# A vision block with attention and routed FFN on one core: joint rotation of two tiles, FFN groups of three chunks, three dispatch scatters in flight, nine serial search rounds

## The chip, the cores and the metric

The kernel runs on one core of one Trainium2 chip. The metric is the device time of one execution in microseconds (us), the median of several runs. Engines are named TensorE (PE; PEld is its weight load), VectorE (DVE), ScalarE (ACT), GpSimd (POOL) and SyncE (SP).

## The reference

64 images of 224 x 224 x 3 become 196 patches each, 12544 tokens of width D = 192. The block embeds the patches, adds attention, and adds an FFN with one shared expert and eight routed ones:

```python
h = patches(x) @ W + b                          # 768 -> 192
n = layernorm(h); q, k = rope(n @ Wq.T), rope(n @ Wk.T); v = n @ Wv.T    # 12 heads of 16
w = where(tril, erf(q @ k.T / 4) + 1, 0)        # per image, 196 x 196
h = h + (w @ v / max(w.sum(-1), 1e-6)) @ Wproj.T
f = layernorm(h); probs = softmax(f @ Wr); top 2 of 8, their weights normalized
capacity = ceil(12544 * 2 / 8 * 1.25)           # the best `capacity` tokens of each expert
routed  = scatter_add(order, (silu(f[order] @ w1) * (f[order] @ w3)) @ w2 * weight)
shared  = (silu(f @ s1) * (f @ s3)) @ s2        # inner width 768
return h + routed + shared
```

`rope` turns neighbouring pairs of a head's 16 channels by an angle that depends on the position.

## The kernel before

The program has three parts in a row, each with its own stream of instructions per engine, written by hand, with semaphores between them; no scheduler moves anything.

**attention()** goes over 32 units of two images (392 tokens, four tiles of 98 rows). Within a unit `turn()` goes over steps n = 0 to 11, one per pair of heads: TensorE makes the scores, ScalarE copies them (L420) and applies gelu (L435), VectorE forms the weights (L549, L556, L608, L564), GpSimd multiplies (L690), TensorE sums over v. Between these steps the next unit is prepared: ScalarE copies the transposed, normalized tokens `normed_t` at n = 3 (L411, behind the gelu of that step), TensorE multiplies tokens of the unit after it (L748) and then q and k of the next (L741), ScalarE copies these to `qk_raw` (L411), and VectorE rotates two of the four tiles at n = 3 and two at n = 4 (L617 to L636). The sum with the projection is at L653, and the bias of the tokens is added once per unit at L663. `by_cos` and `by_sin` hold the products of one tile; two of each take turns. VectorE instructions that read what VectorE wrote just before are set apart by `settle()`, a wait on its own semaphore.

**choices()** does the routing: the top two, and for each expert a search for the threshold at its capacity, in ROUNDS = 15 rounds of three trials. A round is three counts on VectorE (L1069), their sum over the chunks on TensorE (L1052), and the comparison (L926, L1094). SERIAL of the rounds run alone, ahead of the FFN; the rest, a count, and the placing of the tokens (from step PLACING = 18 to step 23) run as steps s of `search_and_place` on VectorE, one behind each pair of inner chunks of the first ROUTING = 5 shared units, beside `add_counts` on TensorE. `R.total` and `R.offset` are its PSUM banks. The last two steps add to `R.placed`.

**ffn()** goes over 25 shared units g of 512 tokens (the last, SHORT, 256) and then 64 routed units of 490 tokens, eight per expert. The inner width 768 is MI = 6 chunks m of 128. `tensor_pair` makes gate and up of two chunks: eight ordinary passes per chunk (L1245 to L1248, float16 in high and low parts), and then the passes of half the rows for both chunks (L1251 and L1253, which run side by side). `tensor_out`, a third of the down projection of the unit before (L1274 to L1276), follows each pair. ScalarE does silu and the high part of hidden (`scalar_unit`, L1290, L1284), VectorE the product and the low part (`vector_unit`, L1309, L1302). `split` prepares tokens of a later unit at chunk `split_at`: for shared units 3, for SHORT and the routed ones 1. Gate and up have two PSUM banks each, so pair p + 1 needs the banks that pair p's chunks leave:

```python
for m in (2 * pair, 2 * pair + 1):
    pe.wait_ge(T.multiplied, MI * g + m + 1)
```

GpSimd writes each token's place into a table by 196 indirect DMAs (L1464), as soon as `R.placed` is 2, with at most two in flight; SyncE loads `ids` from that table after all of them, and GpSimd gathers the rows of the routed units by `ids` (L1476), which `split` (ScalarE L1576, VectorE L1661) turns into high and low parts that a DMA transposes.

## Time and profile before

| | before |
|---|---|
| runs, us | 3378.82, 3384.44, 3385.17 (median 3384.44) |
| profiled execution, us | 3376.83 |
| its span, us | 3374.7 |
| mean granted TensorE clock | 0.945 |
| TensorE busy | 3091.8 us (92%), 25828 instructions |
| VectorE busy | 2446.8 us (73%), 4893 instructions |
| ScalarE busy | 1526.7 us (45%) |
| GpSimd busy | 1377.0 us (41%) |
| chain that ended last | TensorE 44%, VectorE 2%, ScalarE 1%, issue 2% |

Attention takes the span's first 1600 us or so, the serial part of the routing the next hundred, the shared units reach to about 2200 and the routed ones to the end. The busy shares are means over these stages. A row of a timeline gives the start, the duration, the engine, the line, the operation, what is written and read, its form, and in brackets how long the engine was idle before it and what ended that. A row of the waits gives who waited for whom, for how long in total, how often, and the longest. A row of the windows gives the window and its length, then the busy time and the instructions of PE, PEld, DVE, ACT and POOL, then the granted clock, the busy share of the DMA engines and GB/s. The granted clock is given as a share of full speed.

### The profile page before, as it was taken

Reading aid. Unit: us, or ns where it says so; the run is one execution under the profiler, and the core shown is the slowest. Engines: PE = TensorE matmul, PEld = TensorE weight load, DVE = VectorE, ACT = ScalarE, POOL = GpSimd, SP = SyncE. Lnnn points to the kernel's source line nnn. Section 1 sums busy time; section 2 is a strip of 40 time slices with the busy share of each in tenths; the row PEclk is TensorE's granted clock in tenths of the full one; section 3 lists DMA queues with packets and bytes.
Section 4 is the critical chain, followed back from the end, with each engine's and each line's share of the span. In section 5 each row is a group of like instructions: output and inputs, shape, how many; then the busy total and the mean of one; then the engine's idle time right before and its main releaser. Section 6 shows DMA issues by size and latency. Waiting matters only on the chain. (4 is left out here: it accounts for less than half of the span.)

```text
span 3374.7 us, 70939 instructions
## 1 busy us (share of the span) xinstructions
PE 3091.8 (92%) x25828; PEld 2110.6 (63%) x25828; DVE 2446.8 (73%) x4893; ACT 1526.7 (45%) x3223; POOL 1377.0 (41%) x1172
## 2 busy tenths in 40 slices
PE   6999999999999999998059999899999999999997
PEld 5777777777777777766025555556666556566664
DVE  6999999999999999997766555554555455455543
ACT  2444444444444444443024444444555455455443
POOL 1332233223332332322202555536666555655664
PEclk9899999999999999986579999999999999999999
DMA  3333333323332333322122222245554555545442
GB/s 104 77 75 78 73 87 80 81 66 87 89 76 68 81 89 75 75 46 54 45 67 67 74 67 78 59 95 101 77 96 71 98 71 97 101 69 97 77 75 42
DMA packets 460505, 260.36 MB, mean 77 GB/s; under 512 B 337967, under 2 KB 441759, under 8 KB 456063
## 3 DMA queue, kind: packets, MB, share of 16 engines
q1 hardware_dynamic: 392448, 196.41, 24.3%
q0 software_dynamic: 54464, 49.01, 10.3%
q10 hardware_dynamic: 13262, 10.66, 0.9%
q8 instruction: 192, 3.15, 0.4%
q14 instruction: 139, 1.14, 0.1%
HBM read 107.98 MB, written 68.15 MB: 52 GB/s over the span
## 5 line engine op out<-in xcount | busy, mean ns | idle before, releaser
L1309 DVE SCALAR_TENSOR_TENSOR ffn_hidden<-ffn_up,ffn_silu 128x490 f32<-128x490 f32 (+2 forms) x534 | 350.6, 670 | 676.2 <-ACT ffn_silu L1290 510.9
L690 POOL TENSOR_TENSOR weights<-weights,x_pair 128x400 f32<-128x400 f32 x384 | 396.3, 1032 | 828.7 <-DVE weights L556 810.1
L1290 ACT ACTIVATE ffn_silu<-ffn_gate 128x490 f32<-128x490 f32 (+2 forms) x534 | 301.9, 582 | 735.6 <-PE ffn_up L1253 541.6
L1487 POOL DMA_INDIRECT out_rows<-done,ids x256 | 407.4, 1591 | 407.6 <-ACT done L1593 346.4
L608 DVE RECIPROCAL recip<-x_product 128x200 f32<-128x200 f32 x384 | 534.2, 1391 | 0.0
L1274 PE MATMUL ffn_out<-ffn_w_hi,ffn_hidden_hi 128*128 128x192 f16 (+1 forms) x2124 | 525.6, 247 | 3.9 <-DVE ffn_hidden_lo L1302 2.0
L1275 PE MATMUL ffn_out<-ffn_w_lo,ffn_hidden_hi 128*128 128x192 f16 (+1 forms) x2124 | 522.8, 246 | 0.0
L1276 PE MATMUL ffn_out<-ffn_w_hi,ffn_hidden_lo 128*128 128x192 f16 (+1 forms) x2124 | 522.7, 246 | 0.0
L748 PE MATMUL bank<-w_tok,patches 128*128 128x192 f32 x1536 | 327.2, 370 | 56.8 <-ACT normed_t L411 32.7
L1302 DVE TENSOR_TENSOR ffn_hidden_lo<-ffn_hidden,ffn_hidden_hi 128x490 f16<-128x490 f32 (+2 forms) x534 | 356.3, 667 | 15.9
L1284 ACT CAST ffn_hidden_hi<-ffn_hidden 128x490 f16<-128x490 f32 (+2 forms) x534 | 320.7, 601 | 91.9 <-DVE ffn_hidden L1309 90.7
L748 PEld LDWEIGHTS bank<-w_tok,patches 128*128 128x128 f32 x1536 | 290.4, 217 | 72.8 <-ACT normed_t L411 39.2
L1476 POOL DMA_INDIRECT tokens<-dram_x,ids x256 | 279.1, 1090 | 91.1 <-issue 76.2
L420 ACT ACTIVATE x_pair<-score 128x400 f32<-128x400 f32 x384 | 192.5, 502 | 269.2 <-DVE weights L556 180.4
L857 PE MATMUL y_sum<-v_held,weights 128*64 128x68 f32 (+1 forms) x1536 | 262.4, 253 | 31.5 <-DVE weights L564 31.5
L1274 PEld LDWEIGHTS ffn_out<-ffn_w_hi,ffn_hidden_hi 128*128 128x128 f16 (+1 forms) x2124 | 219.2, 103 | 110.3 <-issue 98.5
L1464 POOL DMA_INDIRECT dram_table<-entry,slot_of x196 | 202.9, 1035 | 207.4 <-issue 131.8
L435 ACT ACTIVATE weights<-x_pair 128x400 f32<-128x400 f32 x384 | 205.0, 534 | 182.0 <-PE y_sum L863 177.5
L741 PE MATMUL bank<-w_qkv,normed_t 96*128 96x192 f32 (+1 forms) x1024 | 275.5, 418 | 0.7 <-ACT normed_t L411 0.7
L859 PE MATMUL y_sum<-v,weights 128*64 128x51 f32 (+2 forms) x1536 | 248.3, 244 | 0.0
L1245 PE MATMUL ffn_gate<-ffn_tokens,ffn_w_hi 128*128 128x490 f16 (+2 forms) x534 | 199.8, 374 | 36.3 <-DVE ffn_tokens L1230 12.4
L741 PEld LDWEIGHTS bank<-w_qkv,normed_t 96*128 96x128 f32 x1024 | 180.3, 192 | 68.9 <-issue 4.4
(176 smaller groups left out, 6862.2 us busy)
## 6 DMA issues: line engine op xcount, KB each, us to landing
patches<-in_patches SPq DMA_DIRECT2D x32, 1176.0 KB, 5.2
ffn_raw<-in_w SPq DMA_DIRECT2D x18, 768.0 KB
dram_x_t<-x_t SPq DMA_DIRECT2D x32, 392.0 KB, 3.7
x_t<-dram_x_t SPq DMA_DIRECT2D x24, 512.0 KB
base<-dram_h SPq DMA_DIRECT2D x24, 384.0 KB, 4.2
out_rows<-sums ACTq DMA_DIRECT2D x24, 384.0 KB, 4.6
v_held<-v SPq DMA_DIRECT2D x64, 102.0 KB, 2.3
dram_h<-h SPq DMA_DIRECT2D x32, 192.0 KB
```

What stands on the lines that cost most here:

```text
L608: nc.vector.reciprocal(recip[:, n % 2], x_product[:, n % 2]).then_inc(inverted, 1)
L690: nc.gpsimd.tensor_tensor(weights[:, n % 4], weights[:, n % 4], x_pair[:, n % 4, ::-1], ALU.mult)\
L741: last = nc.tensor.matmul(out, wide(lhs, k, t), rhs[:, k, 0:width], start=(k == 0), stop=(k == 1))
L748: last = nc.tensor.matmul(out, wide(patches[slot], i, n), tok_w[:, i, :], start=(i == 0), stop=(i == KP - 1))
L1274: nc.tensor.matmul(out, hi, w_hi[:, m, :], start=(m == 0), stop=False)
L1275: nc.tensor.matmul(out, hi, w_lo[:, m, :], start=False, stop=False)
L1276: last = nc.tensor.matmul(out, lo, w_hi[:, m, :], start=False, stop=(m == MI - 1))
L1284: nc.scalar.copy(T.hidden_hi[slot][:, m, 0:n], T.hidden[:, m % 2, 0:n]).then_inc(T.hi_ready, 1)
L1290: nc.scalar.activation(T.silu[:, m % 2, 0:n], T.gate[m % 2][:, 0:n], ACT.Silu, scale=1.0 / (TOKEN_SCALE * WEIGHT_SCALE)).then_inc(T.silued, 1)
L1302: nc.vector.tensor_tensor(T.hidden_lo[slot][:, m, 0:n], T.hidden[:, m % 2, 0:n], T.hidden_hi[slot][:, m, 0:n], ALU.subtract).then_inc(T.lo ...
L1309: nc.vector.scalar_tensor_tensor(T.hidden[:, m % 2, 0:n], T.up[m % 2][:, 0:n], HIDDEN_SCALE / (TOKEN_SCALE * WEIGHT_SCALE), T.silu[:, m % ...
L1487: nc.gpsimd.indirect_dma_start(out=dram["out"][:, :], out_offset=bass.IndirectOffsetOnAxis(ap=ids[i][0:height, t, 0:1], axis=0), in_=done[ ...
```

## The change

Six edits:

- **Rotation.** `by_cos` and `by_sin` hold both tiles of a step. Both copies of `qk_raw` are waited for, then one product by cosine and one by sine cover both tiles, then one difference and one sum.
- **Copies ahead of gelu.** At n = 3 ScalarE copies `normed_t` before the gelu of the step.
- **SERIAL** is 9 instead of 11, so that steps 9 to 23 lie behind the 15 pairs of units 0 to 4.
- **Groups.** `tensor_group` and `units_group` take three chunks where no routing step stands (from unit 5 on); gate and up have a third bank each, `R.total` and `R.offset`. Unit 5 waits for `R.placed` first. The down projection comes in halves there, the last one of all in one part. Seven shared units are written out instead of five.
- **Split.** In units with groups of three it stands at chunk 2 (shared), at chunk 5 (SHORT), and ahead of chunk 0 (routed).
- **Dispatch.** FLYING = 3 scatters may be in flight.

```diff
-        by_cos = [sb(f"by_cos{s}", [128, 2 * NH, 2, HD // 2]) for s in range(2)]
-        by_sin = [sb(f"by_sin{s}", [128, 2 * NH, 2, HD // 2]) for s in range(2)]
+        by_cos = sb("by_cos", [128, 2, 2 * NH, 2, HD // 2])
+        by_sin = sb("by_sin", [128, 2, 2 * NH, 2, HD // 2])
...
+                    if n == 3 and has_next:
+                        for k, pos in enumerate(LN1T):
+                            copy_out(pos, normed_t[:, k * UT:(k + 1) * UT], KD)
                     if pairs:
...
                         nc.scalar.activation(weights[:, n % 4], x_pair[:, n % 4], ACT.Gelu, scale=SCORE_SCALE)\
                           .then_inc(gelued, 1)
-                    if n == 3 and has_next:
-                        for k, pos in enumerate(LN1T):
-                            copy_out(pos, normed_t[:, k * UT:(k + 1) * UT], KD)
...
-                        shape = [128, 2 * NH, 2, HD // 2]
+                        t = 2 * (n - 3)
                         for i in range(2):
-                            t = 2 * (n - 3) + i
-                            dve.wait_ge(free[QK[t] % NB], fills(kind, u, QK[t]))
-                            src = qk_raw[:, t, :].rearrange("p (h c f) -> p h c f", h=2 * NH, c=2)
-                            if i == 0:
-                                settle()
-                            step(nc.vector.tensor_tensor(by_cos[i][:], src, over(tables[:, i, 0, :], shape), ALU.mult))
-                            step(nc.vector.tensor_tensor(by_sin[i][:], src, over(tables[:, i, 1, :], shape), ALU.mult))
+                            dve.wait_ge(free[QK[t + i] % NB], fills(kind, u, QK[t + i]))
                         settle()
-                        for i in range(2):
-                            t = 2 * (n - 3) + i
-                            step(nc.vector.tensor_tensor(rotated[:, t, :, 0:HD // 2], by_cos[i][:, :, 0, :],
-                                                         by_sin[i][:, :, 1, :], ALU.subtract))
-                            step(nc.vector.tensor_tensor(rotated[:, t, :, HD // 2:HD], by_cos[i][:, :, 1, :],
-                                                         by_sin[i][:, :, 0, :], ALU.add))
+                        src = qk_raw[:, t:t + 2, :].rearrange("p i (g f) -> p i g f", f=HD // 2)
+                        for c, out in enumerate((by_cos, by_sin)):
+                            table = tables[:, :, c, :].unsqueeze(2).to_broadcast([128, 2, 4 * NH, HD // 2])
+                            step(nc.vector.tensor_tensor(out[:].rearrange("p i h c f -> p i (h c) f"), src, table, ALU.mult))
+                        settle()
+                        step(nc.vector.tensor_tensor(rotated[:, t:t + 2, :, 0:HD // 2], by_cos[:, :, :, 0, :],
+                                                     by_sin[:, :, :, 1, :], ALU.subtract))
+                        step(nc.vector.tensor_tensor(rotated[:, t:t + 2, :, HD // 2:HD], by_cos[:, :, :, 1, :],
+                                                     by_sin[:, :, :, 0, :], ALU.add))
...
-SERIAL = 11
+SERIAL = 9
...
+FLYING = 3
...
+    T.gate.append(R.total)
+    T.up.append(R.offset)
...
+def units_group(g):
+    return 2 if isinstance(g, int) and g < ROUTING else 3
...
+def tensor_group(nc, pe, T, g, slot, ws, n, part, group):
+    chunks = range(group * part, group * part + group)
+    after_pairs = group == 3 and isinstance(g, int) and g == ROUTING
...
-        pe.wait_ge(T.multiplied, MI * g + m + 1)
+        pe.wait_ge(T.multiplied, MI * g + m + 3 - (2 if after_pairs and m < 2 else group))
...
-    share = len(tiles) * MI // 3
-    for k in range(third * share, (third + 1) * share):
+    share = len(tiles) * MI // parts
+    for k in range(part * share, (part + 1) * share):
...
+    if split_at is None:
+        split()
...
-                if n >= 2:
-                    pool.wait_ge(dispatched[n % 2], 16 * (n // 2))
+                if n >= FLYING:
+                    pool.wait_ge(dispatched[n % FLYING], 16 * (n // FLYING))
...
+                if isinstance(g, int) and g == ROUTING:
+                    pe.wait_ge(R.placed, 2)
+                group = units_group(g)
...
-            for part in range(3):
-                tensor_out(nc, pe, T, SHARED + XUNITS - 1, 0, 0, ROUTED, part)
+            tensor_out(nc, pe, T, SHARED + XUNITS - 1, 0, 0, ROUTED, 0, 1)
```

Where the change moves instructions, the order on the engine is shown before and after. On VectorE, one of the two rotation places of a unit, before:

```order
L626 TENSOR_TENSOR by_cos<-qk_raw,rope 128x384
L627 TENSOR_TENSOR by_sin<-qk_raw,rope 128x384
L626 TENSOR_TENSOR by_cos<-qk_raw,rope 128x384
L627 TENSOR_TENSOR by_sin<-qk_raw,rope 128x384
L631 TENSOR_TENSOR rotated<-by_cos,by_sin 128x24x8
L633 TENSOR_TENSOR rotated<-by_cos,by_sin 128x24x8
L631 TENSOR_TENSOR rotated<-by_cos,by_sin 128x24x8
L633 TENSOR_TENSOR rotated<-by_cos,by_sin 128x24x8
L549 SCALAR_TENSOR_TENSOR x_product<-x_pair 128x200
```

The same place after:

```order
L627 TENSOR_TENSOR by_cos<-qk_raw,rope 128x768
L627 TENSOR_TENSOR by_sin<-qk_raw,rope 128x768
L629 TENSOR_TENSOR rotated<-by_cos,by_sin 128x48x8
L631 TENSOR_TENSOR rotated<-by_cos,by_sin 128x48x8
L549 SCALAR_TENSOR_TENSOR x_product<-x_pair 128x200
```

Four instructions stand where eight stood, and the elements they cover are the same. On ScalarE, step n = 3 of a unit (`h_new` are the raw tokens, `x_pair` the scores), before:

```order
L420 ACTIVATE x_pair<-score 128x400
L435 ACTIVATE weights<-x_pair 128x400
L411 COPY normed_t<-bank 96x392 x2
L411 COPY h_new<-bank 128x192
L411 COPY qk_raw<-bank 128x384 x2
```

And after (L438 is the gelu now):

```order
L420 ACTIVATE x_pair<-score 128x400
L411 COPY normed_t<-bank 96x392 x2
L438 ACTIVATE weights<-x_pair 128x400
L411 COPY h_new<-bank 128x192
L411 COPY qk_raw<-bank 128x384 x2
```

The two copies passed the gelu. On TensorE, the end of a pair in a routed unit, before:

```order
L1248 MATMUL ffn_up<-ffn_tokens,ffn_w_hi 128x490
L1251 MATMUL ffn_gate<-ffn_tokens,ffn_w_lo 128x490
L1253 MATMUL ffn_up<-ffn_tokens,ffn_w_lo 128x490
L1251 MATMUL ffn_gate<-ffn_tokens,ffn_w_lo 128x490
L1253 MATMUL ffn_up<-ffn_tokens,ffn_w_lo 128x490
L1274 MATMUL ffn_out<-ffn_w_hi,ffn_hidden_hi 128x192
```

The end of a group after (`total` and `offset` are the third banks of gate and up):

```order
L1261 MATMUL offset<-ffn_tokens,ffn_w_hi 128x490
L1264 MATMUL ffn_gate<-ffn_tokens,ffn_w_lo 128x490
L1266 MATMUL ffn_up<-ffn_tokens,ffn_w_lo 128x490
L1264 MATMUL ffn_gate<-ffn_tokens,ffn_w_lo 128x490
L1266 MATMUL ffn_up<-ffn_tokens,ffn_w_lo 128x490
L1264 MATMUL total<-ffn_tokens,ffn_w_lo 128x490
L1266 MATMUL offset<-ffn_tokens,ffn_w_lo 128x490
L1287 MATMUL ffn_out<-ffn_w_hi,ffn_hidden_hi 128x192
```

Three chunks' half-row passes stand together; there are two such ends per unit instead of three.

## Rows read from the trace of the kernel before

**Rows 1.** Windows: busy time of each engine in two stages.

```profile
200.00:1500.00 1300.00, 1230.93 (x11933) 953.23 (x11931) 1253.14 (x2807) 616.34 (x1410) 393.32 (x381) 0.96 0.33 78
...
2200.00:3300.00 1100.00, 1091.86 (x8070) 657.04 (x8071) 564.92 (x903) 555.82 (x1123) 642.45 (x480) 1.00 0.49 86
```

**Rows 2.** Timeline of VectorE, the rotation of a unit.

```profile
836.06 0.55 DVE L626 TENSOR_TENSOR by_cos<-qk_raw,rope 128x384 f32<-128x384 f32 x1
836.52 0.55 DVE L627 TENSOR_TENSOR by_sin<-qk_raw,rope 128x384 f32<-128x384 f32 x1
...
838.04 0.36 DVE L631 TENSOR_TENSOR rotated<-by_cos,by_sin 128x192 f32<-128x192 f32 x1
838.32 0.35 DVE L633 TENSOR_TENSOR rotated<-by_cos,by_sin 128x192 f32<-128x192 f32 x1
```

**Rows 3.** Timeline of VectorE, one instruction per unit of attention, 128x768.

```profile
821.59 0.95 DVE L663 TENSOR_TENSOR h_new<-h_new,bias 128x768 f32<-128x768 f32 x1
...
868.71 0.94 DVE L663 TENSOR_TENSOR h_new<-h_new,bias 128x768 f32<-128x768 f32 x1
...
917.16 0.95 DVE L663 TENSOR_TENSOR h_new<-h_new,bias 128x768 f32<-128x768 f32 x1
```

**Rows 4.** Timeline of ScalarE, in two units of attention.

```profile
835.09 0.48 ACT L411 COPY qk_raw<-bank 128x384 f32<-128x384 f32 x1 [0.81 <-PE bank L741]
...
876.41 0.53 ACT L435 ACTIVATE weights<-x_pair 128x400 f32<-128x400 f32 x1
...
883.62 0.48 ACT L411 COPY qk_raw<-bank 128x384 f32<-128x384 f32 x1 [0.81 <-PE bank L741]
```

**Rows 5.** Timeline of VectorE, the rotation one unit later.

```profile
883.16 0.55 DVE L626 TENSOR_TENSOR by_cos<-qk_raw,rope 128x384 f32<-128x384 f32 x1
```

**Rows 6.** Waits in attention, 300 to 1400 us (23 units): total, times, longest.

```profile
PE bank L748 <- ACT normed_t L411: 27.6, 23, 1.3
...
DVE h L653 <- PE bank L741: 11.1, 20, 0.6
```

**Rows 7.** Windows at the token products of two units; PEclk is the granted clock.

```profile
829.00:834.00 5.00, 3.83 (x20) 3.08 (x19) 4.93 (x11) 2.10 (x6) 1.95 (x2) 1.00 0.66 241
876.80:880.40 3.60, 3.04 (x10) 3.05 (x11) 3.53 (x8) 0.89 (x3) 1.25 (x2) 0.53 0.69 290
```

**Rows 8.** Timeline of TensorE, two serial search rounds.

```profile
1657.41 0.56 PE L1052 MATMUL total<-count,same 128*128 128x3 f32 x2 [54.33 <-DVE reached L1069]
1662.53 0.59 PE L1052 MATMUL total<-count,same 128*128 128x3 f32 x2 [4.56 <-DVE reached L1069]
```

**Rows 9.** Timeline of VectorE, a search round behind a pair, and what follows.

```profile
1726.11 0.15 DVE L926 TENSOR_SCALAR enough<-total 128x3 int32<-128x3 f32 x1
...
1730.47 0.69 DVE L1309 SCALAR_TENSOR_TENSOR ffn_hidden<-ffn_up,ffn_silu 128x512 f32<-128x512 f32 x1
```

**Rows 10.** Timeline of TensorE, shared unit 2, behind its third pair.

```profile
1782.60 0.39 PE L1057 MATMUL offset<-running,before 128*128 128x8 f32 x2 [3.05 <-DVE running L1076]
```

**Rows 11.** Timeline of TensorE, end of a pair in a routed unit.

```profile
2604.05 0.37 PE L1247 MATMUL ffn_up<-ffn_tokens,ffn_w_lo 128*128 128x490 f16 x1
2604.26 0.37 PE L1248 MATMUL ffn_up<-ffn_tokens,ffn_w_hi 128*128 128x490 f16 x1
2604.56 0.38 PE L1251 MATMUL ffn_gate<-ffn_tokens,ffn_w_lo 64*128 64x490 f16 x1
...
2605.08 0.26 PE L1274 MATMUL ffn_out<-ffn_w_hi,ffn_hidden_hi 128*128 128x192 f16 x1
```

**Rows 12.** The dispatch scatters on GpSimd: ns, first and last start.

```profile
L1464 POOL DMA_INDIRECT dram_table<-entry,slot_of x196: 969/972/1760, 1816.0 to 2178.6; - x196
```

**Rows 13.** Timeline of ScalarE, the last shared unit (SHORT).

```profile
2191.15 0.63 ACT L1576 ACTIVATE split_rows<-tokens 128x512 f16<-128x512 f32 x1 [7.90 <-DMA tokens<-dram_x,ids]
```

**Rows 14.** Timeline of TensorE, the SHORT unit, and the last unit of all.

```profile
2193.75 0.28 PE L1245 MATMUL ffn_gate<-ffn_tokens,ffn_w_hi 128*128 128x256 f16 x1 [4.36 <-issue]
...
3347.31 0.24 PE L1274 MATMUL ffn_out<-ffn_w_hi,ffn_hidden_hi 128*128 128x192 f16 x1 [1.82 <-DVE ffn_hidden_lo L1302]
```

More of the change, by code:

```diff
@@ L1164, in ffn_weights, with ffn_units @@
     return T
[L1167 removed]
+def ffn_units(ctx, nc, T, R):
     def sb(name, shape, dt=F32):
@@ L1248, in tensor_pair, with tensor_out @@
             nc.tensor.matmul(out, hi[:, beyond], far, start=False, stop=False)
-    for m in (2 * pair, 2 * pair + 1):
+    for m in chunks:
         beyond = slice(INNER + m * 128, INNER + (m + 1) * 128)
-        nc.tensor.matmul(T.gate[m % 2][:, 0:n], T.w_lo[ws][0][top, beyond], far[top], start=False, stop=True)\
+        nc.tensor.matmul(T.gate[m % group][:, 0:n], T.w_lo[ws][0][top, beyond], far[top], start=False, stop=True)\
           .then_inc(T.gated, 1)
-        nc.tensor.matmul(T.up[m % 2][:, 0:n], T.w_lo[ws][1][low, beyond], far_again[low], start=False, stop=True)\
+        nc.tensor.matmul(T.up[m % group][:, 0:n], T.w_lo[ws][1][low, beyond], far_again[low], start=False, stop=True)\
           .then_inc(T.gated, 1)
-def tensor_out(nc, pe, T, g, slot, ws, tiles, third):
-    if third == 0:
+def tensor_out(nc, pe, T, g, slot, ws, tiles, part, parts):
+    if part == 0:
         pe.wait_ge(T.lo_ready, MI * g + MI + 2)
@@ L1299, in vector_unit @@
 def vector_unit(nc, dve, T, g, slot, n, split, split_at, behind_pair=None):
+    group = units_group(g)
     def lo(m):
@@ L1303, in lo @@
                                 ALU.subtract).then_inc(T.lo_ready, 1)
+    if split_at is None:
+        split()
     for m in range(MI):
@@ L1321, in shared_units @@
 def shared_units(eng, unit):
-    for g in range(ROUTING):
+    ahead = ROUTING + 2
+    for g in range(ahead):
         unit(g, g // 2, g % 2, WHOLE)
-    with eng.Fori(0, (SHARED - 2 - ROUTING) // 2) as j:
-        unit(2 * j + ROUTING, j + ROUTING // 2, 1, WHOLE)
-        unit(2 * j + ROUTING + 1, j + ROUTING // 2 + 1, 0, WHOLE)
+    with eng.Fori(0, (SHARED - 2 - ahead) // 2) as j:
+        unit(2 * j + ahead, j + ahead // 2, 1, WHOLE)
+        unit(2 * j + ahead + 1, j + ahead // 2 + 1, 0, WHOLE)
     unit(SHARED - 2, (SHARED - 3) // 2, 1, WHOLE)
@@ L1378, in ffn @@
                 "xt_in", "base_in", "sums_out", "rows_in", "scattered", "routed_in"))
-        dispatched = [sem(f"dispatched{k}") for k in range(2)]
+        dispatched = [sem(f"dispatched{k}") for k in range(FLYING)]
         ids_in = [sem(f"ids_in{i}") for i in range(8)]
@@ L1414, in _ @@
                 sp.dma_start(ids[i][XR:XR16, 3, :], dram["pads"]).then_inc(pads_in, 16)
-            for k in range(2):
-                sp.wait_ge(dispatched[k], 16 * PER)
+            for k in range(FLYING):
+                sp.wait_ge(dispatched[k], 16 * len(range(k, 2 * PER, FLYING)))
             for i in range(4):
@@ L1529, in unit @@
                 pe.wait_ge(T.tokens_lo, 2 * g + 6)
-                for part in range(3):
-                    tensor_pair(nc, pe, T, g, slot, 0, columns_of(tiles), part)
+                if isinstance(g, int) and g == ROUTING:
+                    pe.wait_ge(R.placed, 2)
+                group = units_group(g)
+                for part in range(MI // group):
+                    tensor_group(nc, pe, T, g, slot, 0, columns_of(tiles), part, group)
                     if isinstance(g, int) and g < ROUTING:
@@ L1534, in unit @@
                     if not (isinstance(g, int) and g == 0):
-                        tensor_out(nc, pe, T, g - 1, 1 - slot, 0, WHOLE, part)
+                        tensor_out(nc, pe, T, g - 1, 1 - slot, 0, WHOLE, part, MI // group)
             shared_units(pe, unit)
```

33 lines of the change are left out of this document (16 added, 17 removed).

## The prediction

> **What bounds the kernel now.** I read the busy shares of the engines by stage first, then each stage's longest engine in the timeline, then who waits for whom. The kernel has three stages with different limits [rows 1]. In attention (200 to 1500 us) VectorE is busy 1253 of 1300 us and TensorE 1231: VectorE leads, TensorE is close behind. In the routed units (2200 to 3300) TensorE is busy 1092 of 1100, and VectorE has half its time free. Between the two lie the routing and the first shared units, where TensorE stands and VectorE's search sets the pace [rows 8 to 10]. So the parts of the change pay by different rules: an instruction saved on VectorE counts in attention, a pass saved on TensorE counts in the FFN, a serial round counts whole.
>
> The profiled execution took 3376.83 us; the median of the three runs, 3384.44, lies 7.6 above it. The sum is made in differences, which I put on the median. Two measurements of this kernel cannot tell less than about 0.2% (6.8 us) from no change.
>
> **Rotation on VectorE.** Before, one of the two rotation places of a unit is four products of 384 elements and four sums of 192. Products start 0.46 apart though each is 0.55 long, so the next starts before the last is done; sums start 0.28 apart [rows 2]. Afterwards there are two products of 768 and two sums of 384. The trace has an instruction of 768 elements, 0.945 long [rows 3]; less the same overlap it takes about 0.86. So two products turn from 0.93 into 0.86 and two sums from 0.55 into 0.47: 0.15 per pair of instructions merged, and with two such merges (cosine and sine; difference and sum) 0.30 per place, 0.60 per unit. That is the gain where VectorE never waits.
>
> It does wait in every other unit. Units alternate: 821.59 to 868.71 is 47.1, 868.71 to 917.16 is 48.5 [rows 3]. In the long kind TensorE's granted clock is 0.53 around the token products, against 1.00 at the same place of the short kind [rows 7], and VectorE then waits for the projection; over 23 units these waits are 11.1 us in 20 pieces [rows 6]. In a long unit what VectorE saves becomes more of that wait. What shortens it is the other edit in attention: ScalarE copies the normalized tokens ahead of the gelu instead of behind it. TensorE waits for those copies once per unit, 27.6 us over 23 units, 1.2 each [rows 6]; the gelu in front takes 0.53, less the tenth by which ScalarE's instructions overlap [rows 4]. So the long unit gains about 0.4. The gelu comes later by two copies; GpSimd, its user, then waits for VectorE's weights anyway, so I cost that at nothing.
>
> The merged product needs both copies of qk_raw at its start, where before the first was enough. In the short kind the second copy ends at 835.57 and VectorE comes at 836.06 [rows 2, 4]: no wait. In the long kind it ends at 884.10 and VectorE came at 883.16 [rows 4, 5]: a new wait of 0.94, less the 0.4 by which the copies come earlier, 0.5. What is queued behind it on VectorE is the rest of the unit, up to the projection's sum, where 0.5 is what it has waited anyway. So I take it as absorbed.
>
> Mean gain (0.6 + 0.4)/2 = 0.5 for each of 31 units that prepare a next one: **-16**. Bounds: -40 where both kinds gain fully, +7 where all units become the long kind less 0.4 (48.05 against a mean of 47.8).
>
> The VectorE rows weigh against a rule. The Trainium skill, page "VectorE: DVE Perf Modes", section "The DRAIN you can't avoid", says that the next instruction does not start until the pipe has emptied; its section on the TRN2 errata gives (N+151)/0.96 ns for a float32 tensor_tensor, so that each instruction removed would be worth 0.157 us, 0.63 per place and 1.26 per unit. The lengths in the trace agree with that formula, the starts do not agree with the first sentence.
>
> **Nine serial rounds instead of eleven.** A serial round is 5.12 us, with TensorE idle for 4.56 of it [rows 8]: 2 x 5.12 = 10.2 gone. The two rounds go behind pairs of a shared unit, where one costs VectorE 4.36 us [rows 9], between its own FFN work. Everything behind them slips by two pairs: placing starts in unit 3 instead of unit 2, and its last step lies behind unit 4's last pair. The stall for placing, 3.05 us [rows 10], should mostly go, since the placing then starts behind a unit's first pair, with no split of tokens ahead of it. Two new stalls come: about 3 us for the two extra full rounds, and a wait ahead of unit 5, because groups of three need the PSUM banks of the routing. VectorE's last placing step stands in front of that wait; behind the wait TensorE holds unit 5's first group, and ScalarE and VectorE wait for that. I take 4. Net given back 3.7, so **-6.5**; bounds -10 (all hidden) and -1.5 (both rounds fall fully on TensorE: 8.7).
>
> **Groups of three.** Ordinary passes start 0.21 apart. From the last of them to the first down product it is 0.82, with one ordinary and two half-row passes in it, 3 x 0.21 = 0.62: changing to half rows and back costs 0.20 per group [rows 11]. Groups: 5 x 3 for the units with routing and 84 x 2 for the others (20 shared, 64 routed), instead of 89 x 3. 84 fewer x 0.20 = **-16.8**. The down products and other passes stay in number. The cover of the rest: three chunks are 24 ordinary passes, 5 us of TensorE, and ScalarE (556 of 1100 us) and VectorE (565) are half free there [rows 1], so hidden should be ready in time; if it is not, each late chunk shows as a TensorE wait for ffn_hidden. Bounds: -20 to -8 (if half of it comes back as waits at group ends). The split of the next routed tokens moves to the head of the unit; it waits for gathered rows that today land before it is due, and TensorE has one whole group to work on meanwhile.
>
> **Three scatters in flight, and the way into the routed units.** The 196 scatters run from 1816 to 2178.6, 1.85 apart, of which the instruction itself takes 0.97 [rows 12]; GpSimd waits for landings the rest, and they end after the shared units. With three in flight the gap should fall to some 1.3 to 1.55, and they end 60 to 100 us earlier (196 times 0.3 to 0.5). What follows is short: ScalarE stands 7.90 for gathered rows [rows 13] and TensorE 4.36 in the SHORT unit [rows 14]. Those go. But the split now comes at that unit's last chunk, and the transposes behind it, covered today by what is left of SHORT, lie open. I take **-2** (-8 to +3). The last unit's down projection in one part lets TensorE run up to the last chunk; of its wait of 1.82 [rows 14] I take **-1**.
>
> Sum: -16 - 6.5 - 16.8 - 2 - 1 = -42.3. The profile should take about 3334, and the median 3384.4 - 42.3 = **3342**.
>
> **Rivals.**
> 1. *The clock fall of the long units disappears.* TensorE idles 0.4 less before the token products, and stays at 1.00 there. Then all units are of the short kind: 47.1 - 0.6 = 46.5 instead of 47.8, -40 over 31 units, 24 below my term: 3318. For it: only one kind shows the fall. Against: TensorE waits as long in both kinds, so that wait alone does not explain the fall. 0.20.
> 2. *VectorE's pipe empties between instructions*, so that a merge is worth 0.157 instead of 0.07: 1.26 x 31 = -39, also about 3319. The starts of rows 2 speak against it. 0.05. (By the rule named above.)
> 3. *Attention gives nothing.* TensorE is busy 95% there; if its chain bounds both kinds, or 0.5 of new wait eats the gain, only the FFN terms stay: -26, 3358. For it: TensorE's share. Against: in the short kind VectorE does not wait. 0.18.
> 4. *The merged rotation waits for the second copy in every unit* and the wait is not absorbed. Place: VectorE at the rotation; price 0.94 on a long unit: 48.45 - 0.4 + 0.94 = 49.0 in both kinds, +1.2 x 31 = +37, 53 above my term: 3395, slower. It decides once VectorE arrives more than 0.5 earlier than today in the short kind, which is that kind's slack [rows 2, 4]. 0.05.
> 5. *Dispatch was hidden anyway, and the boundary gets worse* (open transposes, split stuck at the head of units): +3 instead of -2, and the groups give 8 instead of 17: 3356. 0.07.
>
> **How the numbers follow.** My forecast has 0.45. The range goes from 3313 (rival 1 with the better end of the boundary) to 3366 (attention at its upper bound of +7 with the other terms as taken lies at 3365); only rival 4 and the joint ends of several terms lie outside. Faster by over 0.2%: 0.92, within 0.03, slower 0.05.
>
> **What would show it.** Rotation: eight instructions of rows 2 become four, at 0.86 and 0.47 start to start; the alternation 46.5 and 48.0; a wait before the long unit's products of about 0.5. Routing: nine serial rounds of 5.12; a TensorE wait of 3 to 5 us ahead of unit 5; no stall of 3 us in unit 2. Groups: six passes of half rows in a row, routed units 0.2 shorter (two groups in place of three). Dispatch: last scatter before 2120. Boundary: no ScalarE wait of 7.9 for rows, a TensorE wait for transposed tokens instead. I am wrong if a unit of attention takes over 47.8 in the mean, or if routed units show waits for ffn_hidden.

## The result, and the profile after

The changed kernel takes 3571.34 us (3559.75 to 3588.90 in four runs) against 3381.63 before: 1.0567 times as long, 95% interval 1.0517 to 1.0617. It is slower by 190, where 42 less was forecast.

| | before | after |
|---|---|---|
| profiled execution, us | 3376.83 | 3588.90 |
| its span, us | 3374.7 | 3587.1 |
| mean granted TensorE clock | 0.945 | 0.913 |
| TensorE busy | 3091.8 (92%) | 3134.0 (87%) |
| VectorE busy, instructions | 2446.8, 4893 | 2430.2, 4637 |
| end of attention (last sum over v) | 1583.3 | 1582.8 |
| start of shared unit 0 | 1716.4 | 1705.5 |
| start of shared unit 5 | 1823.4 | 1818.9 |
| start of shared unit 8 | 1878.1 | 2108.8 |
| start of the last shared unit, SHORT | 2170.2 | 2397.1 |
| start of the first routed unit | 2200.2 | 2427.6 |
| start of the last routed unit | 3327.6 | 3539.8 |

The starts are those of each unit's first gate matmul. From one row to the next the difference between the kernels is -0.5, -10.4, +6.4, +235.2, -3.8, +0.5 and -15.2: all of the loss lies in shared units 5, 6 and 7, which took 30.8, 167.2 and 91.9 us instead of 18.2. The windows of the changed kernel show that stretch as the third row (columns as in [rows 1]):

```profile
200.00:1500.00 1300.00, 1239.27 (x11968) 958.71 (x11967) 1243.36 (x2597) 617.61 (x1413) 393.86 (x382) 0.96 0.34 78
1800.00:1840.00 40.00, 33.21 (x233) 19.25 (x231) 23.16 (x39) 15.04 (x27) 13.94 (x14) 0.96 0.21 67
1840.00:2098.00 258.00, 75.07 (x205) 20.41 (x205) 18.84 (x30) 14.72 (x26) 179.69 (x182) 0.54 0.05 11
2098.00:2400.00 302.00, 302.00 (x2206) 182.59 (x2206) 166.93 (x265) 137.99 (x247) 0.97 (x1) 0.99 0.21 69
2500.00:3300.00 800.00, 793.74 (x5958) 492.00 (x5956) 413.61 (x658) 409.86 (x832) 472.57 (x362) 1.00 0.51 89
```

Around it TensorE is as busy as it was [rows 1]; in it, it is busy for 75 of 258 us at half clock, VectorE for 19, the DMA engines for 5%. GpSimd alone works on: it issues the dispatch scatters. Three of its rows, from the timeline:

```profile
1901.39 0.97 POOL L1488 DMA_INDIRECT dram_table<-entry,slot_of  x1 [0.30 <-issue]
1902.67 0.97 POOL L1488 DMA_INDIRECT dram_table<-entry,slot_of  x1 [0.30 <-issue]
1903.94 0.97 POOL L1488 DMA_INDIRECT dram_table<-entry,slot_of  x1 [0.30 <-issue]
```

They follow each other every 1.28 us for up to 24 in a row, where two in flight had a mean of 1.86 [rows 12] and came at most two in a row. With the pauses that GpSimd makes between these rows, its own semaphore and register instructions among them (60 of 366 beside the slow units take over 0.5 us, most of them 0.70 to 0.73, where they take 0.02 or 0.03 in e1_two below), the mean is 1.43. TensorE's timeline nearby:

```profile
1863.07 0.59 PE L1258 MATMUL ffn_gate<-ffn_tokens,ffn_w_hi 128*128 128x512 f16 x1 [2.21 <-issue]
1865.87 0.59 PE L1259 MATMUL ffn_gate<-ffn_tokens,ffn_w_hi 128*128 128x512 f16 x1 [2.21 <-issue]
1868.67 0.59 PE L1260 MATMUL ffn_gate<-ffn_tokens,ffn_w_lo 128*128 128x512 f16 x1 [2.21 <-issue]
1871.47 0.59 PE L1261 MATMUL ffn_gate<-ffn_tokens,ffn_w_hi 128*128 128x512 f16 x1 [2.21 <-issue]
```

These are ordinary passes of one chunk, 0.21 apart in [rows 11], here 2.80 apart, with no wait for data: "issue" alone. Of the 145 starts beside the scatters that come over 0.65 us after the one before, 127 lie close to 0.7, 1.4, 2.1 or 2.8. SyncE, which only issues DMAs, has one issue of 1.40 us that takes 0.37 after the last scatter (2098):

```profile
2047.30 1.40 SPq L1421 DMA_DIRECT2D base<-dram_h  x1
...
2112.17 0.37 SPq L1421 DMA_DIRECT2D base<-dram_h  x1
```

It has only four issues in the stretch, and the other three took 0.69, 0.37 and 0.01, so SyncE alone would show little.

TensorE's first such gap comes at 1837.7, 18 us after the first scatter (1819.8), beside the ninth of an unbroken row that began at 1827.3. The granted clock is still 1.00 then; it falls at 1842.4, behind the first three late starts.

The other parts, by their lines. The rotation, in a unit where VectorE waits (first two rows) and in one where it does not:

```profile
694.29 0.37 DVE L564 SCALAR_TENSOR_TENSOR weights<-weights,causal 128x264 f32<-128x264 f32 x1
695.43 0.96 DVE L627 TENSOR_TENSOR by_cos<-qk_raw,rope 128x768 f32<-128x768 f32 x1 [0.78 <-issue]
...
742.87 0.94 DVE L627 TENSOR_TENSOR by_cos<-qk_raw,rope 128x768 f32<-128x768 f32 x1
743.73 0.95 DVE L627 TENSOR_TENSOR by_sin<-qk_raw,rope 128x768 f32<-128x768 f32 x1
744.72 0.56 DVE L629 TENSOR_TENSOR rotated<-by_cos,by_sin 128x384 f32<-128x384 f32 x1
745.20 0.55 DVE L631 TENSOR_TENSOR rotated<-by_cos,by_sin 128x384 f32<-128x384 f32 x1
```

The merged products start 0.86 apart and the sums 0.48, as taken. The wait of 0.78 is for the second copy, which ScalarE ends at 695.35:

```profile
694.87 0.48 ACT L411 COPY qk_raw<-bank 128x384 f32<-128x384 f32 x1 [0.81 <-PE bank L739]
```

The waits in attention, 300 to 1400 us (total, times, longest), against [rows 6]:

```profile
PE bank L746 <- ACT normed_t L411: 13.8, 22, 0.8
...
DVE by_cos L627 <- issue: 10.8, 10, 1.7
...
DVE h L651 <- PE bank L739: 8.3, 13, 0.6
```

TensorE's wait for the normalized tokens is halved; a wait of VectorE at the rotation is new, 10.8 us in 10 units; the wait at the projection fell from 11.1 only to 8.3.

The first unit of the FFN and unit 5, where TensorE now waits 4.85 for the placing:

```profile
1705.46 0.59 PE L1258 MATMUL ffn_gate<-ffn_tokens,ffn_w_hi 128*128 128x512 f16 x1 [12.46 <-DVE ffn_tokens L1233]
...
1818.86 0.58 PE L1258 MATMUL ffn_gate<-ffn_tokens,ffn_w_hi 128*128 128x512 f16 x1 [4.85 <-DVE slot_of L1083]
```

The end of a group in a routed unit:

```profile
2800.00 0.37 PE L1261 MATMUL offset<-ffn_tokens,ffn_w_hi 128*128 128x490 f16 x1
2800.30 0.38 PE L1264 MATMUL ffn_gate<-ffn_tokens,ffn_w_lo 64*128 64x490 f16 x1
...
2800.72 0.37 PE L1264 MATMUL total<-ffn_tokens,ffn_w_lo 64*128 64x490 f16 x1
...
2801.03 0.26 PE L1287 MATMUL ffn_out<-ffn_w_hi,ffn_hidden_hi 128*128 128x192 f16 x1
```

The turn to half rows and back stays at 0.3 on each side, as in [rows 11], once per three chunks: routed units take 17.53 instead of 17.74, shared ones 18.02 instead of 18.23.

### The profile page after: what moved, and what is told of

Same layout as the page of the kernel before. It is cut to its first block, busy times and chain, and to the rows that moved or that the text cites. A ratio compares the mean times of both kernels' runs of the same rounds, so it can differ in the third digit from the quotient of the medians.

```text
span 3587.1 us, 70594 instructions
## 1 busy us (share of the span) xinstructions
PE 3134.0 (87%) x25828; PEld 2135.0 (60%) x25828; DVE 2430.2 (68%) x4637; ACT 1528.3 (43%) x3223; POOL 1351.9 (38%) x1172
## 4 chain that ended last, share of the span: by engine, by line
PE 43%; issue 6%; DVE 2%; ACT 1%; POOL 0%; DMA 0%; ACTq 0%; DVEq 0%; POOLq 0%
PE ffn_out L1287 5%; PE ffn_out L1288 5%; PE ffn_out L1289 5%; PE ffn_gate L1264 2%; PE ffn_gate L1258 2%; PE ffn_gate L1259 2%; PE ffn_up L1258 2%; PE ffn_gate L1261 2%; PE ffn_gate L1260 2%; PE ffn_up L1259 2%; PE ffn_up L1260 2%; PE ffn_up L1261 2%; PE offset L1261 1%; PE offset L1259 1%; PE total L1258 1%
## 5 line engine op out<-in xcount | busy, mean ns | idle before, releaser
L1332 DVE SCALAR_TENSOR_TENSOR ffn_hidden<-ffn_up,ffn_silu 128x490 f32<-128x490 f32 (+2 forms) x366 | 237.9, 670 | 721.0 <-ACT ffn_silu L1308 469.7
L1308 ACT ACTIVATE ffn_silu<-ffn_gate 128x490 f32<-128x490 f32 (+2 forms) x366 | 204.0, 582 | 913.9 <-PE ffn_up L1266 526.0
L1288 PE MATMUL ffn_out<-ffn_w_lo,ffn_hidden_hi 128*128 128x192 f16 (+1 forms) x2124 | 525.7, 247 | 46.6 <-issue 46.6
L1511 POOL DMA_INDIRECT out_rows<-done,ids x256 | 405.3, 1583 | 419.8 <-ACT done L1620 358.5
L1500 POOL DMA_INDIRECT tokens<-dram_x,ids x256 | 265.7, 1038 | 387.6 <-DMA ids<-dram_table 307.5
L438 ACT ACTIVATE weights<-x_pair 128x400 f32<-128x400 f32 x384 | 205.6, 536 | 182.0 <-PE y_sum L861 177.4
L1288 PEld LDWEIGHTS ffn_out<-ffn_w_lo,ffn_hidden_hi 128*128 128x128 f16 (+1 forms) x2124 | 219.9, 104 | 56.6 <-issue 56.5
L1289 PEld LDWEIGHTS ffn_out<-ffn_w_hi,ffn_hidden_lo 128*128 128x128 f16 (+1 forms) x2124 | 219.7, 103 | 56.9 <-issue 56.8
L1488 POOL DMA_INDIRECT dram_table<-entry,slot_of x196 | 194.6, 993 | 127.3 <-issue 122.2
```

The source lines that it names most:

```text
L1288: nc.tensor.matmul(out, hi, w_lo[:, m, :], start=False, stop=False)
L1289: last = nc.tensor.matmul(out, lo, w_hi[:, m, :], start=False, stop=(m == MI - 1))
L1500: nc.gpsimd.indirect_dma_start(out=rows[slot][0:height, t, :], out_offset=None, in_=dram["x2"][:, :], in_offset=bass.IndirectOffsetOnAxis( ...
L1511: nc.gpsimd.indirect_dma_start(out=dram["out"][:, :], out_offset=bass.IndirectOffsetOnAxis(ap=ids[i][0:height, t, 0:1], axis=0), in_=done[ ...
```

## The experiments

Theory R says that scatters which follow each other without a break slow the issue of the other engines. The rivals blame code that runs for the first time, the third PSUM bank, three in flight as such, or what the scatters write. In the table, "excess" is the time from the start of shared unit 5 to that of SHORT above 19 steady units (18.02 each, 18.23 where pairs stand); "step" is from the start of SHORT to the first routed unit. Starts of the scatters are from the timelines. "One" marks a version that ran once; scatters, excess and step are from one profile each. With nine serial rounds unit 5 takes 1.4 to 2.9 us more than a steady unit even where TensorE never falls behind, so an excess of that size does not show a loss by the scatters.

| run | scatters: first to last, mean distance | excess | step | time, us |
|---|---|---|---|---|
| before | 1816 to 2179, 1.86 | 0.4 | 30.0 | 3381.6 |
| changed | 1820 to 2098, 1.43 | 236 | 30.5 | 3571.3 |
| e1_two | 1805 to 2163, 1.84 | 3.0 | 35.6 | 3350.4 |
| e2_before_three | 1816 to 2090, 1.40 | 242 | 27.8 | 3615.7 (one) |
| e3_paced | 1808 to 2264, 2.34 | 2.9 | 134 | 3446.5 (one) |
| e4_late | 1894 to 2173, 1.43 | 238 | 29.6 | 3587.3 (one) |
| e5_spaced2 | 1805 to 2091, 1.46 | 183 | 29.8 | 3520.6 (one) |
| e6_spaced4 | 1809 to 2111, 1.55 | 143 | 29.7 | 3479.7 |
| e10_threes | 1809 to 2202, 2.02 | 1.6 | 72.3 | 3384.2 (one) |
| e12_nines | 1803 to 2131, 1.68 | 48 | 29.4 | 3376.8 |
| e13_sixes | 1814 to 2166, 1.80 | 4.5 | 29.6 | 3350.5 |
| e15_fives11 | 1803 to 2174, 1.90 | 0.0 | 43.4 | 3358.5 |
| e9_serial11 | 1801 to 2165, 1.87 | 0.7 | 35.3 | 3347.6 |
| e14_quarter | 1806 to 2080, 1.41 | 236 | 30.5 | 3573.3 (one) |
| e11_gather | 1807 to 2084, 1.42 | 237 | 30.0 | 3576.3 (one) |

**Two in flight.**

```diff
-FLYING = 3
+FLYING = 2
```

> The changed kernel with two scatters in flight, all else as changed. Theory R (scatters that follow each other every 1.28 us slow the other engines' issue; units 5 to 7 took 30.8, 167 and 92 us instead of 18): units 5 to 7 take 18 to 20 us each, the 236 us of excess go, and the time falls to about 3571 - 236 = 3335 to 3355, some 25 to 45 below before. Theory U (the cause is the code written out for units 5 and 6 or the third PSUM bank, and the scatters are bystanders): units 5 to 7 stay at 30 to 170 us and the time above 3520.

Measured 3350.35, ratio 0.9907 (0.9878 to 0.9937); units 5 to 7 took 19.6, 18.0 and 18.0. With the one number turned back the other five edits gain 32 us. The scatters' row (ns; first and last start):

```profile
L1488 POOL DMA_INDIRECT dram_table<-entry,slot_of x196: 964/971/1832, 1805.3 to 2163.4; - x196
```

**The kernel before with three in flight**, the same lines of GpSimd and SyncE as in the change, nothing else.

> The kernel before with three scatters in flight, nothing else. Theory R: scatters every 1.28 us from 1816 on, over within 280 us, and the shared units meanwhile take 30 to 170 us instead of 18.2; time 3550 to 3620. Theory U: shared units stay at 18.2, the scatters end near 2080, time within 10 us of before.

Measured 3615.7, units 5 and 6 at 147 and 132 us:

```profile
L1466 POOL DMA_INDIRECT dram_table<-entry,slot_of x196: 966/971/1225, 1815.9 to 2089.5; - x196
```

The scatters alone make the loss; it needs neither the written-out units nor the third bank nor the groups.

**A pause behind each scatter.**

```diff
...
+                nc.gpsimd.memset(pace[:], 0.0).then_inc(paced, 1)
+                pool.wait_ge(paced, n + 1)
+                pool.sem_inc(spacer, 1)
```

> The changed kernel, three scatters in flight, but a memset of 128x256 and a wait for it behind each scatter, so that they start some 1.7 us apart. If the rate of the scatters is what hurts: units 5 to 7 near 18 us, time 3335 to 3360. If the number allowed in flight hurts whatever the rate: units 5 to 8 take 30 to 170 us again, time above 3500.

The distance came out at 2.3, not 1.7, since the wait for the memset costs 0.97. No unit is slow. The scatters end 112 us after SHORT has begun, and the step of 134 us is TensorE waiting for them; so 3446 lies in neither range, though the units are as the rate has them.

**A later start.**

```diff
+            pool.wait_ge(T.lo_ready, MI * 9 + 2)
+            pool.sem_inc(spacer, 1)
```

> The changed kernel, three scatters in flight back to back, but the first one waits until shared unit 9 is done, when the loop over the shared units has been through its body once on every engine. Theory R: the units that lie beside the scatters are slow whatever code they run: three or four units of 30 to 170 us, total excess near 236 us, time 3550 to 3600. Theory F (only code that has to be fetched for the first time is slowed): the units stay at 18 us, the scatters end by about 2180, time 3340 to 3360.

The same excess, now in units 10 and 11 (168 and 104 us), in code that every engine had run before. The Trainium skill, page "Runtime: NRT & Kernel Launch", section "Instruction fetch mechanics", has each engine load its instructions in blocks by its own DMA queue, mostly hidden. Code loaded for the first time was therefore a suspect; this run clears it.

**Other instructions between the scatters.**

```diff
...
+                for _ in range(2):
+                    pool.sem_inc(paced, 1)
```

(e6_spaced4: `range(4)`.)

> The changed kernel, three scatters in flight, two register-like instructions of 0.08 us behind each scatter, so that they follow at 1.44 us instead of 1.28. Theory T (the other engines fall behind only where scatters come faster than something drains them, and the limit of two was the brake: its mean was 1.85): between 1.28 and 1.85 there is a threshold; if it lies above 1.44, units 5 to 7 take 30 to 170 us again and the time is above 3480; if below, they take 18 and the time is 3335 to 3355. Theory C (three allowed in flight hurts by itself): slow in either case.

> As the run before, with four such instructions, 1.6 us from scatter to scatter. Theory T: no slow unit (18.0 from unit 6 on), last scatter near 2120 instead of 2163, the step from shared to routed units 30 instead of 35.6, time 3340 to 3350, at or up to 6 below the version with two in flight (3350). Theory C: slow units, above 3480.

Both missed what they were made for. The median distance stayed at 1.28; the small instructions run ahead while GpSimd works on a scatter. The means of 1.46 and 1.55 come from pauses in between. The loss falls with the mean (183, 143), which suits both theories.

**Rows of three, nine, six and five.** GpSimd waits until all scatters before have landed, ahead of every third:

```diff
-                if n >= FLYING:
-                    pool.wait_ge(dispatched[n % FLYING], 16 * (n // FLYING))
-                    pool.sem_inc(spacer, 1)
+                if n >= FLYING and n % FLYING == 0:
+                    for k in range(FLYING):
+                        pool.wait_ge(dispatched[k], 16 * (n // FLYING))
+                        pool.sem_inc(spacer, 1)
```

The others wait like this ahead of every ninth, sixth or fifth, and keep the limit of three between these pauses.

> The changed kernel, three scatters back to back, then a wait until all three have landed, and so on: three in flight at their peak, but a mean distance near that of two in flight (1.8 to 2.0 us). Theory T (the mean rate decides; 1.55 us still cost 143 us, two in flight at 1.85 cost nothing): units 5 to 15 at 18 to 20 us, time 3345 to 3365. Theory C (a third scatter in flight is what hurts): units of 25 us and more wherever scatters run, time above 3450.

```profile
L1488 POOL DMA_INDIRECT dram_table<-entry,slot_of x196: 964/972/1831, 1809.3 to 2202.3; - x196
```

```profile
1850.00:2050.00 200.00, 200.00 (x1464) 120.48 (x1463) 111.69 (x176) 92.80 (x165) 97.99 (x97) 1.00 0.24 74
```

TensorE is busy for all of 1850 to 2050. Three in flight do no harm when a pause follows; theory C falls. The pauses are too many, so the scatters end at 2202, the routed units wait, and 3384 misses theory T's range.

> The changed kernel, three scatters in flight, but ahead of every ninth scatter a wait until all before it have landed (about 3 us). Theory B (the other engines fall behind only after an unbroken row of scatters: TensorE's first gaps came 17 us, 13 scatters, after the first; a pause drains what has piled up): no slow units, mean distance (8 x 1.28 + 4) / 9 = 1.6, last scatter near 2120, the step from shared to routed units 30, time 3338 to 3350, up to 10 below the version with two in flight. Theory T2 (the mean rate decides, and 1.6 is too fast): units of 25 to 45 us, time above 3400.

```profile
L1491 POOL DMA_INDIRECT dram_table<-entry,slot_of x196: 969/974/1465, 1802.9 to 2130.5; - x196
```

```profile
1850.00:2050.00 200.00, 187.20 (x1316) 109.85 (x1314) 100.37 (x157) 83.85 (x150) 119.41 (x119) 0.97 0.23 66
```

> As the run before, with the wait ahead of every sixth scatter: mean distance (5 x 1.28 + 4) / 6 = 1.75, last scatter near 2150. Both theories: no slow units if rows of nine have none; the step from shared to routed units 30 to 33, time 3342 to 3352. If rows of nine are slow and rows of six are not, the limit lies between the two.

By the length of the row, rows of 2 or 3 scatters leave an excess of 3.0 or less, rows of 6 leave 4.5 (four starts of TensorE over 0.65 us after the one before), rows of 9 leave 48 (35 such starts), and unbroken ones 236 (145). The mean distance puts the runs into the same order (4.5 or less from 1.80 up, 48 at 1.68, 143 at 1.55, 183 at 1.46), so the sums alone do not tell the two theories apart. What speaks for the row is where in it TensorE falls behind. Of the 35 late starts with rows of nine, 25 come behind the ninth scatter of a row, eight behind the eighth, two behind the seventh and none behind the first six; with rows of six all four come behind the sixth. One end of a row of nine (the scatter at 1891.21 is the ninth, the next one stands behind the pause):

```profile
1891.21 0.97 POOL L1491 DMA_INDIRECT dram_table<-entry,slot_of  x1 [0.30 <-issue]
1896.82 0.97 POOL L1491 DMA_INDIRECT dram_table<-entry,slot_of  x1 [4.63 <-DMA dram_table<-entry,slot_of]
...
1891.03 0.24 PE L1289 MATMUL ffn_out<-ffn_w_hi,ffn_hidden_lo 128*128 128x192 f16 x1 [1.09 <-issue]
1891.77 0.24 PE L1287 MATMUL ffn_out<-ffn_w_hi,ffn_hidden_hi 128*128 128x192 f16 x1 [0.50 <-issue]
1893.16 0.24 PE L1288 MATMUL ffn_out<-ffn_w_lo,ffn_hidden_hi 128*128 128x192 f16 x1 [1.15 <-issue]
1893.90 0.24 PE L1289 MATMUL ffn_out<-ffn_w_hi,ffn_hidden_lo 128*128 128x192 f16 x1 [0.50 <-issue]
1893.98 0.24 PE L1287 MATMUL ffn_out<-ffn_w_hi,ffn_hidden_hi 128*128 128x192 f16 x1
```

Rows of nine were expected to be free and are not: 12 of the 22 reach late starts at their end, and the pause then ends them. Theory T2 expected over 3400, which did not come either. Something that fills within a row and drains in the pause fits all of this; no run shows what it is, and none has long rows at a mean of 1.85 or short ones at 1.5. Rows of nine took 3376.77 (ratio 0.9982, 0.9965 to 0.9998), rows of six 3350.51 (0.9918, 0.9891 to 0.9944).

**A quarter of the rows**, and **reading instead of writing.**

```diff
-                    out_offset=bass.IndirectOffsetOnAxis(ap=slot_of[:, n:n + 1], axis=0),
-                    in_=entry[:, 2 * n:2 * n + 2], in_offset=None, bounds_check=SLOTS - 1, oob_is_err=False)\
+                    out_offset=bass.IndirectOffsetOnAxis(ap=slot_of[0:32, n:n + 1], axis=0),
+                    in_=entry[0:32, 2 * n:2 * n + 2], in_offset=None, bounds_check=SLOTS - 1, oob_is_err=False)\
```

> The changed kernel, three scatters in flight, unbroken, but each writes 32 rows instead of 128 (left out: the places of three tokens in four, so the routed part works on fewer tokens and on spare rows). Theory K (what piles up is the work per row: descriptors, writes): a quarter of the load, units 5 to 8 at 18 to 20 us, time 3330 to 3360. Theory I (what piles up is per instruction or per completion, whatever it moves): units of 30 to 170 us again, excess of 150 us or more.

```profile
L1488 POOL DMA_INDIRECT dram_table<-entry,slot_of x196: 860/866/1130, 1805.9 to 2080.3; - x196
```

```profile
1850.00:2050.00 200.00, 65.86 (x152) 15.23 (x151) 10.27 (x16) 8.52 (x15) 123.87 (x143) 0.50 0.03 7
```

> The changed kernel, but the 196 dispatch transfers read rows of 8 bytes from the table into a tile of their own instead of writing rows of 8 bytes into the table (so the table stays empty and the routed part works on spare rows). Same instruction, same three in flight, same 128 rows. Theory D (making descriptors on GpSimd at that rate is what hurts): units 5 to 7 at 30 to 170 us as in the changed kernel. Theory M (the small writes into device memory are what hurts): units at 18 us, whole time 3330 to 3360.

```profile
L1489 POOL DMA_INDIRECT found<-dram_table,slot_of x196: 992/998/1299, 1806.8 to 2084.0; - x196
```

Excess 236 and 237, as with the full scatters. It depends neither on how many rows an indirect DMA moves (one took 866 ns instead of 971) nor on whether device memory is read or written. What is left is something that goes by the instruction or by its completion; the runs do not show which.

**The attention edits apart**, each on top of e1_two: the copies behind the gelu again (joint rotation alone), and the rotation tile by tile again (copies alone).

> The version with two scatters in flight, with the copies of the normalized tokens behind the gelu again, so that of the attention edits the joint rotation stands alone. Theory W (the joint product waits for the second copy in the units with the clock fall, 0.75 to 1.7 us in the changed kernel, and that wait is added): without the earlier copies the wait grows by 0.4, the long units take 48.6 to 49.5, the short ones 46.6, attention ends at 1575 to 1590 (1568 with the copies, 1583 before), time 3355 to 3370. Theory A (the wait is absorbed at the projection, as predicted): long units 48.4, attention ends near 1573, time about 3352 to 3358.

> The version with two scatters in flight, with the rotation tile by tile again, so that of the attention edits the earlier copies stand alone. Both theories: no wait at the rotation, short units 47.1, long ones 48.0, so attention ends 5 to 10 before 1583 and the time is 3353 to 3362. If the earlier copies make the clock fall rarer, more units are short and it ends earlier than that; if they do nothing it ends at 1583.

Measured 3365.93 (0.9962, 0.9948 to 0.9976) and 3363.26 (0.9955, 0.9939 to 0.9972). Attention ends at 1581.9 and 1579.9 (with the copies alone 5 to 10 before 1583 was expected). With neither edit it ends at 1583.3 and 1582.8 (before, e2_before_three), with both at 1565.3 to 1582.8 in thirteen profiles, 1571.6 in the mean. The waits of the rotation alone, 300 to 1400 us:

```profile
PE bank L746 <- ACT normed_t L411: 27.4, 23, 1.3
...
DVE by_cos L627 <- issue: 11.3, 11, 1.2
...
DVE h L651 <- PE bank L739: 11.3, 23, 0.6
```

The new wait is 11.3 us in 11 units. The wait at the projection is still 11.3 in all, but it lies elsewhere: before, a long unit had two of 0.47 and 0.64 there and a short one none; now a long one has 0.64 and a short one some 0.37. So in a long unit (48.6, as before) a new wait of about 1.05 took the place of 0.47, and in a short one (47.0, where theory W had 46.6) most of what the merging saved became a wait. Time and end are as theory W has them, the short units as neither has. By its one profile each edit alone gives 1 to 3 us, both together 12 in the mean.

**Eleven serial rounds**, on top of e1_two.

```diff
-SERIAL = 9
+SERIAL = 11
```

> The version with two scatters in flight and eleven serial rounds instead of nine. By the trace of the changed kernel the two rounds behind pairs took the FFN's first unit 11 us earlier and gave back 6.4 by unit 5, among it 6.6 on the wait for the placing ahead of unit 5. If that is the whole of it, this version is 4 to 5 us slower than with nine: 3353 to 3357. Rival: with eleven the placing is done some 10 us earlier in unit 4, the scatters start as early and the way into the routed units is the same or shorter: no difference, 3347 to 3353.

3347.63 (0.9903, 0.9884 to 0.9921), the same as with nine. From the end of attention to unit 5 it takes 6.9 us longer (243.3 against 236.4), yet the scatters start at the same distance (235.9 and 237.3), because the placing ends two pairs earlier: the last step lies behind unit 4's first pair, not behind its last. And it is the scatters that set the rest: with two in flight the first routed unit starts 21.6 to 22.1 us after the last scatter in before, e1_two, e7_rotation, e8_copies and e9_serial11 alike.

**All together**: eleven rounds, three in flight, a pause ahead of every fifth.

> The version that the runs point to: eleven serial rounds, three scatters in flight with a pause ahead of every fifth, all else as changed. From the versions with two in flight (3348 and 3350): the scatters start near 1803, mean distance (4 x 1.28 + 4) / 5 = 1.85, or 1.7 if the pauses are shorter, last one near 2140 to 2160, the step to the routed units 30 instead of 35. Expected 3340 to 3350. If the pauses cost what the missing limit gains, 3346 to 3354, the same as with two in flight.

3358.45 (0.9948, 0.9931 to 0.9965), above both ranges: excess 0, but the mean distance was 1.90 and the step 43 us, so the pauses cost more than the limit of two. The best versions are the change with two in flight, with nine or with eleven serial rounds; rows of six (3350.51) cannot be told apart from them.

## Why the prediction was wrong

- **The step that failed** is "With three in flight the gap should fall to some 1.3 to 1.55, and they end 60 to 100 us earlier". The gap fell to 1.28 and they ended 80 earlier, but the step counted only what the scatters wait for, and nothing that they do to others. Beside them TensorE's matmuls started 0.7 to 2.8 us apart instead of 0.21, and units 5 to 7 took 235 us longer. No rival had scatters at GpSimd's full rate slow another engine, so 3571 lay outside every case. The limit of two, which the prediction read as a fault, was the brake: it kept the longest unbroken row at two, and the mean distance at 1.86.
- **"What follows is short ... I take -2"**: +0.5 was measured in the change, where nothing waited for scatters any more; there the step of 30 has other owners: TensorE stands 6.55 for hidden within SHORT and 8.52 ahead of the first routed unit. But the end of the scatters is no short matter once the units ahead are faster: in e1_two it gave back 5.6 us of what attention and groups had gained.
- **Rotation, -16**: -0.5 in the profiled execution, -12 in the mean of thirteen. The sizes were nearly right (0.86 and 0.48; short units 46.6, long ones 48.3, against 46.5 and 48.0 forecast). Mis-sized was the wait at the second copy, for which 0.5 was taken and "So I take it as absorbed" written: it was 0.75 to 1.7. In a long unit about as much as was taken was absorbed (of the two waits at the projection the one of 0.47 went, the one of 0.64 stayed), and the rest was added. Wrong, too, was that the kinds of units would go on alternating: in the change long units follow each other, and there are kinds of 47.5 (the wait at the projection alone) and of 49.2 (a wait of 1.7 at the rotation). From run to run the mix differs, and with it 17 us. Rival 1 (no clock fall) and rival 4 (the wait in every unit) are both there, in some units each.
- **The clock fall**: the prediction saw a clock fall in the long units only; in the kernel before, from 300 us on, each unit of either kind has one of some 3.4 us, the short kind right at its start (822.3), the long kind at the token products (876.9). In the change the kind goes with the place of the fall: units of 46.6 have none or one at their start, those of 48.3 one that begins 8.2 to 8.7 us into the unit, those of 47.5 one of 6.8 us at their start, and those of 49.2 one of 6.8 us that begins 6.7 us into it. What moves the fall from run to run is open.
- **Rule and row**: a place takes 3.10 us to the next instruction (742.87 to 745.97) where it took 3.37, so that each of the four instructions removed gave 0.07 and not 0.157. The measurement goes against that sentence of the Trainium skill ("VectorE: DVE Perf Modes", "The DRAIN you can't avoid") where no wait stands between two instructions; the section itself adds that an instruction that is not held starts earlier, which is what these rows show.
- **Nine rounds, -6.5**: -4 up to unit 5, by 10.4 saved and 6.4 given back; the wait ahead of unit 5 was 4.85 where 4 was taken, the stall for placing shrank to 0.58, and so the net was mis-sized at 3.7. Not seen was that none of it reaches the end while the scatters set it.
- **Groups, -16.8**: -3.8 in the shared units from 8 on and -15.2 in the routed ones, of which 63 x 0.21 = 13.2 by the units' own length; 0.21 per group where 0.20 was taken.
- **Tail, -1**: nothing; 25.8 us from the last unit's start to TensorE's end in both.

Without the scatters the sum was -40; the version with two in flight came out 32 below before.

## What to carry to other kernels

A limit on transfers in flight may be what keeps an engine from disturbing the others; before it is lifted, ask what else runs at that engine's full rate, and look at the start times of engines that have nothing to do with it. In a chain of "this many transfers, then that", a saving ahead of the chain's start counts and one beside it does not. A merged instruction needs all of its inputs at once: price the wait for the last of them where the engine arrives early.

## What the runs showed of the hardware

- Indirect DMAs that GpSimd issues every 1.28 us slow TensorE's issue from the sixth to the ninth of a row on: many of its matmuls then start some 0.7, 1.4, 2.1 or 2.8 us apart instead of 0.08 to 0.21. Behind rows of six or nine the pause ends it; without such pauses it goes on to the last scatter, with semaphore and register instructions of GpSimd itself at 0.70 us. From the last one on (2098 to 2400 in the windows) TensorE is busy all the time. Over 196 transfers rows of two or three cost at most 3.0 us, rows of six 4.5, rows of nine 48.
- It does not depend on 32 or 128 rows per transfer, on reading or writing, on code that is new or in a loop (236, 237 and 238 us).
- TensorE's granted clock is 0.54 in that stretch, mostly its lower level, so that what it does issue is slow as well. The fall (1842.4) came behind the first late starts and did not bring them.
- What the engines share there (their instruction supply, the completions, the recording of the profile) was not tried and stays open. Loads of instructions that take long are not seen: the two DMA queues that bring them moved six blocks between 1840 and 2098, none in more than 1.30 us, as elsewhere in the kernel (up to 1.33 between 1500 and 1700).
